# One transformer layer on one core: scores for the exponentials in four column tiles, and an order that keeps products of one kind together

## The reference, cut to what matters

```python
x = x + attention(layernorm(x))      # below
x = x + ffn(layernorm(x))            # ffn: fp4_linear(silu(gate) * up), width 704

# attention, per batch element and head
q, k = rope(xn @ Wq.T + bq), rope(xn @ Wk.T + bk);  v = xn @ Wv.T + bv
att = where(causal, q @ k.T / 4, -inf)          # 2048 x 2048
y = softmax(att) @ v
return concat_heads(y) @ Wo.T + bo
```

## Time and profile before

| | |
|---|---|
| median of 3 runs | 1375.17 us (1373.97 to 1376.26) |
| the profiled execution: its time | 1375.57 us |
| its span, first to last instruction | 1373.7 us |
| PE busy | 1315.7 us, 96% of the span |
| DVE busy | 1094.7 us, 80% |
| ACT busy | 792.5 us, 58% |
| POOL busy | 471.4 us, 34% |
| mean granted TensorE clock | 0.981 of full speed |

### The profile page before, as it was taken

How to read it: one execution, slowest core, us unless ns; L and a number is a source line. 1 busy time by engine, 2 the same in 40 slices (tenths; PEclk the granted TensorE clock), 3 DMA queues, 4 the chain that set the end, 5 groups by cost and what they waited for, 6 DMA issues and landing times.

```text
span 1373.7 us, 22507 instructions
## 1 busy us (share of the span) xinstructions
PE 1315.7 (96%) x8310; PEld 678.8 (49%) x8310; DVE 1094.7 (80%) x2242; ACT 792.5 (58%) x1691; POOL 471.4 (34%) x499
## 2 busy tenths in 40 slices
PE   7689899999999999999999999999999999999977
PEld 6455455454545554444355565555553445533345
DVE  5799889888887988787548988898888888896156
ACT  5346567765555556556775455545457665577821
POOL 2954535444342233320014566233420022300145
PEclk9779999999999999999999999999999999999989
DMA  4723222212101101010023221111101010000000
GB/s 103 185 69 93 67 66 78 55 41 53 40 5 35 32 16 32 9 29 5 25 63 85 55 70 37 29 31 39 32 9 28 24 32 12 13 2 1 9 12 16
DMA packets 56905, 56.18 MB, mean 41 GB/s; under 512 B 10062, under 2 KB 50384, under 8 KB 56784
## 3 DMA queue, kind: packets, MB, share of 16 engines
q1 hardware_dynamic: 55496, 53.66, 14.5%
q10 hardware_dynamic: 1300, 1.08, 0.3%
HBM read 37.55 MB, written 16.78 MB: 40 GB/s over the span
## 4 chain that ended last, share of the span: by engine, by line
PE 83%; DVE 10%; POOL 3%; issue 2%; ACT 1%; DMA 1%; ACTq 0%; SPq 0%; POOLq 0%; DVEq 0%
PE bank L891 18%; PE bank L870 16%; PE bank L852 16%; PE bank L903 12%; PE bank L1023 5%; PE bank L963 4%; DVE piece_max L1267 3%; PE bank L856 2%; PE bank L873 2%; PE bank L971 2%; PE bank L1014 1%; PE bank L898 1%; PE bank L985 1%; DVE c_mem L1347 1%; DVE c_mem L1339 1%
## 5 line engine op out<-in xcount | busy, mean ns | idle before, releaser
L1167 ACT ACTIVATE prob<-bank 128x512 f32<-128x512 f32 (+3 forms) x1280 | 610.2, 539 | 302.4 <-PE bank L870 164.2
L1267 DVE TENSOR_REDUCE piece_max<-bank 128x1 f32<-128x512 f32 (+3 forms) x1120 | 699.6, 664 | 70.1 <-PE bank L852 39.6
L852 PE MATMUL bank<-k_mem,q_mem 96*128 96x512 bf16 (+3 forms) x1280 | 396.9, 352 | 8.3 <-DVE piece_max L1267 6.9
L870 PE MATMUL bank<-q_mem,k_mem 99*128 99x512 bf16 (+3 forms) x1280 | 390.5, 351 | 3.5 <-DMA q_mem<-max_rows 1.6
L891 PE MATMUL bank<-prob,V 128*32 128x512 f32 (+3 forms) x2560 | 300.8, 542 | 2.0 <-ACT prob L1167 0.5
L852 PEld LDWEIGHTS bank<-k_mem,q_mem 96*128 96x128 bf16 x1280 | 122.3, 98 | 185.7 <-issue 103.8
L870 PEld LDWEIGHTS bank<-q_mem,k_mem 99*128 99x128 bf16 x1280 | 121.1, 98 | 180.7 <-issue 97.8
L1475 POOL TENSOR_TENSOR c_mem<-c_mem 128x256 f32<-128x256 f32 (+2 forms) x74 | 84.6, 1143 | 360.5 <-DVE c_mem L1351 360.5
L873 PE MATMUL bank<-mask_kq,ident_h 128*128 128x128 bf16 x512 | 105.0, 220 | 0.0
L856 PE MATMUL bank<-mask_qk,ident_h 128*128 128x128 bf16 x512 | 101.1, 224 | 0.0
L891 PEld LDWEIGHTS bank<-prob,V 128*32 128x32 f32 x2560 | 50.6, 108 | 99.6 <-issue 78.3
(11 more groups left out here) (174 smaller groups left out, 1409.3 us busy)
## 6 DMA issues: line engine op xcount, KB each, us to landing
parts_dram<-a_mem SPq DMA_DIRECT2D x13, 512.0 KB, 3.5
q_mem<-parts_dram SPq DMA_DIRECT2D x32, 192.0 KB, 3.0
k_mem<-parts_dram SPq DMA_DIRECT2D x32, 192.0 KB, 3.5
q_mem<-parts_dram SPq DMA_DIRECT2D x32, 128.0 KB, 3.1
k_mem<-parts_dram SPq DMA_DIRECT2D x32, 128.0 KB, 3.5
c_mem<-in_L_attn_x SPq DMA_DIRECT2D x30, 128.0 KB, 2.0
out<-c_mem SPq DMA_DIRECT2D x30, 128.0 KB, 1.7
a_mem<-in_L_attn_x SPq DMA_DIRECT2D x13, 256.0 KB, 3.0
```

The source lines that it names most:

```text
L852: m = pe.matmul(o, q_rows(u)[0:TERM_ROWS, h, i * P:(i + 1) * P], k_rows(k0 // CHUNK, g)[0:TERM_ROWS, h, k0 % CHUNK:k0 % CHUNK + keys], sta ...
L870: mm = pe.matmul(b[:, off:CHUNK], k_rows(j // TPC, g)[:, h, (j % TPC) * P:(j % TPC + 1) * P], q_rows(u)[:, h, off:CHUNK], start=True, stop ...
L1167: act.activation(prob[:, n % NP, off:CHUNK], bank_of("st", n)[:, off:CHUNK], ACT.Exp, scale=SCALE).then_inc(drained("st", n)[0], 1)
L1267: dve.tensor_reduce(piece_max[:, u % 2, h0:h0 + len(heads), slot], src.rearrange("p (h k) -> p h k", k=keys), AX.X, ALU.max).then_inc(drai ...
```

## The change

The scores for the exponentials are no longer one matmul with 128 weight columns, but four with 32 columns, each to its own 32 partitions of the same bank, the form that the values already have. Their masks are four too, each as wide as the last key of its quarter needs (32, 64, 96 and 128 columns of queries). The scores for maxima stay as they were. In the plan, a job of TensorE now says whether it is "divided" (exponential scores and values are, everything else isn't); a job of the other kind than the last costs 96 ns more; values cost 26 ns beside their columns instead of 235; and among jobs that could begin at once, one of the same kind as the last counts as ready 2,000 ns sooner. The cost of a score in the plan is unchanged.

```diff
--- before.py
+++ after.py
@@ -23,6 +23,8 @@
 TERM_ROWS = sum(terms for _, terms in RUNS) * HD
 ROWS = TERM_ROWS + SPLIT
 GROUP = 4
+
+COLUMNS = 32
 NGROUPS = HEADS // GROUP
 MASKED = -1.0e30
 LN_EPS = 1e-5
@@ -40,8 +42,9 @@
 HANDOVER_NS = dict(pe=195, act=200, dve=145, pool=150, sp=0, aq=0)
-DMA_TURN_NS, DMA_NS, DMA_KB_PER_NS, PV_TURN_NS = 460, 1500, 0.2, 235
+DMA_TURN_NS, DMA_NS, DMA_KB_PER_NS, DIVIDE_NS, BESIDE_NS = 460, 1500, 0.2, 96, 2000
 SOONER_NS = dict(a=0, w=0, xn=10000, s=200, st=0, pv=-100, place=1000, norm=200, c=(0, -2000), tile=1000)
 
 
@@ -77,18 +80,18 @@
         self.at, self.end, self.engine_free, self.begun = {}, {}, {}, {}
         self.bank, self.turn, self.turns = {}, {}, {b: 0 for b in banks}
         self.spare, self.bank_free = list(banks), {b: 0.0 for b in banks}
-        self.jobs, self.now, self.running, self.moved = [], 0.0, None, 0.0
+        self.jobs, self.now, self.running, self.moved, self.divided = [], 0.0, None, 0.0, False
 
     def start(self, job, sooner=0.0):
 
-        self.jobs.append([self.now, sooner, job, (None, [], None), 0.0])
+        self.jobs.append([self.now, sooner, job, (None, [], None, False), 0.0])
 
     def wait(self, names=(), until=None):
-        yield None, list(names), until
+        yield None, list(names), until, False
 
     def load(self, queue, name, kbytes, after=()):
 
-        yield queue, list(after), None
+        yield queue, list(after), None, False
         self.move(queue, name, kbytes, after)
 
     def move(self, queue, name, kbytes, after=()):
@@ -96,12 +99,15 @@
         self.moved = max(self.moved, self.engine_free[queue]) + kbytes / DMA_KB_PER_NS
         self.end[name] = self.moved + DMA_NS
 
-    def step(self, engine, name, ns, after=(), shares=False):
-
-        yield engine, list(after), None
-        self.do(engine, name, ns, after, shares)
-
-    def do(self, engine, name, ns, after=(), shares=False):
+    def step(self, engine, name, ns, after=(), shares=False, divided=False):
+
+
+        yield engine, list(after), None, divided
+        self.do(engine, name, ns, after, shares, divided)
+
+    def do(self, engine, name, ns, after=(), shares=False, divided=False):
+        if engine == "pe" and divided != self.divided:
+            ns, self.divided = ns + DIVIDE_NS, divided
         since = self.running[4] if self.running else 0.0
         begin = max([self.engine_free.get(engine, 0.0), since] + [self.end[a] for a in after])
         if shares and self.begun.get("pool", 0.0) <= begin < self.engine_free.get("pool", 0.0):
@@ -111,16 +117,16 @@
         self.engine_free[engine] = begin + ns
         self.end[name] = begin + ns + HANDOVER_NS[engine]
 
-    def through(self, use, ns, engine, drain_ns, after=(), drain_after=(), first=None):
-
-        yield "pe", list(after), lambda: self.spare
+    def through(self, use, ns, engine, drain_ns, after=(), drain_after=(), first=None, divided=False):
+
+        yield "pe", list(after), lambda: self.spare, divided
         b = min(self.spare, key=lambda b_: self.bank_free[b_])
         self.spare.remove(b)
         self.bank[use], self.turn[use] = b, self.turns[b]
         self.turns[b] += 1
         free = ("bank", b, self.turn[use])
         self.end[free] = self.bank_free[b]
-        self.do("pe", use, ns, [*after, free])
+        self.do("pe", use, ns, [*after, free], divided=divided)
         self.start(self.drain(use, b, engine, drain_ns, drain_after, first), self.running[1])
 
     def drain(self, use, b, engine, ns, after, first):
@@ -136,11 +142,11 @@
         self.spare.append(b)
 
     def can_go(self, job):
-        _, names, until = job[3]
+        names, until = job[3][1:3]
         return all(name in self.end for name in names) and (until is None or until())
 
     def ready(self, job):
-        engine, names, until = job[3]
+        engine, names, until, _ = job[3]
         ends = [job[0]] + [self.end[name] for name in names]
         if engine is None and until:
             ends.append(self.now)
@@ -151,6 +157,8 @@
     def goes(self, job):
         ready = self.ready(job)
         sooner = job[1]() if callable(job[1]) else job[1]
+        if job[3][0] == "pe" and self.divided == job[3][3]:
+            sooner += BESIDE_NS
         return max(ready, self.engine_free.get(job[3][0], 0.0)), ready - sooner
 
     def run(self, over=lambda: False):
@@ -379,15 +387,15 @@
                 yield from plan.wait([("place", u, 2), ("key ones", c)] + room
                                      + ([("drain", "st", n - ST_IN_FLIGHT)] if n >= ST_IN_FLIGHT else []))
                 yield from plan.through(("st", n), 0.43 * (CHUNK - off) + 59 * (j >= c * TPC), "act",
-                                        52 + 0.833 * (CHUNK - off), [("place", u, 2)], room)
+                                        52 + 0.833 * (CHUNK - off), [("place", u, 2)], room, divided=True)
 
     def rehearse_values():
         for m, (u, j, off) in enumerate(steps):
             k, g = units[u]
             of = k - k % NCHUNKS + j // TPC
-            yield from plan.step("pe", ("pv", m), 1.67 * (CHUNK - off) + PV_TURN_NS,
+            yield from plan.step("pe", ("pv", m), 1.67 * (CHUNK - off) + 26,
                                  [("drain", "st", GROUP * m + 3), ("drain", "v", (of * TPC + j % TPC) // PAIR)]
-                                 + ([("o copy", u - 1)] if j == 0 and u else []))
+                                 + ([("o copy", u - 1)] if j == 0 and u else []), divided=True)
             if m == final_step[u]:
                 yield from plan.step("act", ("o copy", u), 493, [("pv", m)] + ([("oT", u - 1)] if u else []))
                 plan.start(rehearse_normalising(u), SOONER_NS["norm"])
@@ -867,10 +875,14 @@
                         at.wait_ge(key_ones_loaded[j // TPC], 16)
                         masked = j >= c * TPC
                         b = take("st", n)
-                        mm = pe.matmul(b[:, off:CHUNK], k_rows(j // TPC, g)[:, h, (j % TPC) * P:(j % TPC + 1) * P],
-                                       q_rows(u)[:, h, off:CHUNK], start=True, stop=not masked)
-                        if masked:
-                            mm = pe.matmul(b[:, off:off + P], ident_h[:, :], mask_kq[:, :], start=False, stop=True)
+                        for k0 in range(0, P, COLUMNS):
+                            first = (j % TPC) * P + k0
+                            mm = pe.matmul(b[k0:k0 + COLUMNS, off:CHUNK], k_rows(j // TPC, g)[:, h, first:first + COLUMNS],
+                                           q_rows(u)[:, h, off:CHUNK], start=True, stop=not masked)
+
+                        for k0 in range(0, P if masked else 0, COLUMNS):
+                            mm = pe.matmul(b[k0:k0 + COLUMNS, off:off + k0 + COLUMNS], ident_h[:, k0:k0 + COLUMNS],
+                                           mask_kq[:, 0:k0 + COLUMNS], start=False, stop=True)
                         mm.then_inc(filled("st", n)[0], 1)
 
             def values():
@@ -888,7 +900,7 @@
                         at.wait_ge(o_copied, u)
                     for h in range(GROUP):
                         v0 = (g * GROUP + h) * VW
-                        mm = pe.matmul(O[32 * h:32 * h + 32, off:CHUNK], V[:, of % V_SLOTS, j % TPC, v0:v0 + 32],
+                        mm = pe.matmul(O[COLUMNS * h:COLUMNS * (h + 1), off:CHUNK], V[:, of % V_SLOTS, j % TPC, v0:v0 + 32],
                                        prob[:, (GROUP * m + h) % NP, off:CHUNK],
                                        start=(j == 0), stop=(m == final_step[u]), skip_group_check=True)
                     mm.then_inc(pv_added, 1)
```

## The result

| | before | after |
|---|---|---|
| median, us | 1375.57 (1373.97 to 1376.26) | 1416.41 (1416.14 to 1422.54) |
| ratio, 95% interval | | 1.0309 (1.028 to 1.0339) |
| profiled execution's span, us | 1373.7 | 1420.7 |
| mean granted clock of TensorE | 0.981 | 0.967 |
| runs of tile form, counted from TensorE's order of instructions | 343 | 383 |

The kernel became 3.1% slower, 41 us. The profiled execution of after is the longest of its four, 6 us above their median, so its rows show a little too much. A "run" here is a stretch of tile-form products on TensorE with no whole-array product between them, as in the prediction; executions of a kernel are not meant. The runs count every stretch of products with at most 32 weight columns, transposes of the maxima included, in the whole kernel.

What follows compares the result with a forecast made beforehand. The prediction took dense TensorE to bound the mixed stretches and ScalarE those where scores run alone. Its only term, (329 - 282) runs x 0.23 us = +10.8 us, gave 1386 us; 8-in-10 range 1360 to 1418.

Steps and rivals of the forecast that it cites:

- mixed stretches: 60 to 675 and 708 to 1256 us: all work mixed, TensorE dense; a microsecond added there costs nearly one.
- the step of 2.07 us unchanged where scores run alone: 675 to 708 and 1256 to 1312 us: ScalarE's four exponentials set each step's pace, before and after.
- A score in four tiles costs its columns: Exponential scores: four tiles stream at once, so 512 columns still take 0.217 us.
- The bound of +54 us: Upper bound if each of 1,280 scores and 512 masks waits 0.03 us for weights; nothing was taken.
- Supply of instructions at nothing: 5,376 more loads and matmuls priced at nothing; rival at 0.06 us a pair: +164 us, 1550, chance 0.06 including tiles not streaming together.
- The price of a turn, 0.23 us: Each tile-form run on TensorE: about 0.10 us in, 0.10 out, 0.03 once for first weights.
- R: Number of tile-form runs in mixed stretches: 282 now, estimated 329 after, from 3.4 pieces for each whole-array run.
- the ring: At most three scores in flight, so a run of scores alone ends after three.
- gain nothing: 38 steps of ScalarE-bound stretches: lose turns, about 9 us of TensorE time, which TensorE then waits.
- Fragments: Rival: waits and narrow diagonal steps cut runs to 2.5 scores, +39 us, 1414; chance 0.09 shared with VectorE dry.
- VectorE dry: Rival: VectorE loses 0.1 us in each of 329 tile runs, +33 us on top, 1419; chance 0.09 shared with Fragments.
- Longer runs: Rival: runs of a whole step or more, 4.5 scores giving 1368 us, 5.25 giving 1360; chance 0.33.

Runs made afterwards that it cites:

- the fastest kernel: The changed kernel with waiting steps also given the 2,000 ns, four scores of each kind in flight, and maxima transposes called divided: 1359.82 us, ratio 0.9893.
- the tie mended: The changed kernel, but in the plan jobs that only wait for something get the 2,000 ns too: 1395.05 us, ratio 1.0154.
- the two orders of 1451 and 1456 us: The 1359.82 us kernel with 1,000 ns instead of 2,000: 1451.32 us; the kernel before with four scores of each kind in flight: 1456.03 us.

## Why the prediction was right in direction and wrong in size

The forecast was +10.8 us; it became +41. The time lies inside the wide range and outside the likeliest case's own (1379 to 1400). The step that failed is "TensorE as dense as before in the mixed stretches, and the step of 2.07 us unchanged where scores run alone": the sum had turns as its only term and put at nothing what the new order makes late. TensorE's idle time rose from 58.0 to 88.3 us and its busy time at the lower clock from 34.0 to 69.1, which cost some 30 and 17.5 us of the 47 between the profiled executions.

- **A score in four tiles costs its columns: right.** The kernel with only the order changed and after itself have the same time (1416.77 and 1416.41). The bound of +54 us is out. Three pairs of kernels have the same order and differ in form alone: 489 runs more and +92.6 us, 33 more and -0.4, 73 fewer and -10.5. With 0.19 us a run and nothing for the form they would be +93, +6 and -14.
- **Supply of instructions at nothing: right.** A dense place of the fastest kernel, four products of 32 weight columns at each row:

```profile
562.29 0.24 PE L882 MATMUL bank<-q_mem,k_mem 99*32 99x128 bf16 x4
562.36 0.23 PE L886 MATMUL bank<-mask_kq,ident_h 128*32 128x32 bf16 x4
562.39 0.26 PE L882 MATMUL bank<-q_mem,k_mem 99*32 99x128 bf16 x4
```

  The eight products of the first two rows start within 0.10 us (562.29 to 562.39), with their loads, 0.013 us each against the rival's 0.06. It isn't only a burst: 64 in a row, from 1233.62 us of this kernel on, start 0.024 us apart. The rule of 62 ns in the Trainium skill ("TensorE: Matmul & The Clock Gate", Part 1) isn't seen in any of the runs.
- **The price of a turn, 0.23 us: right to a fifth.** 0.19 over 489 runs with nothing else changed, 0.14 over 73. Where the order changes with the number, the quotient is anything from 0.04 (2,000 to 500 ns) to 0.31 (500 to 0 ns), because the order's own cost is in it.
- **R: too low.** The 343 and 383 are of the whole kernel. Counted as the forecast did, in mixed stretches and without the runs that are transposes of maxima alone, before has 281 (282 in the forecast) and after 365, not 329: 3.1 pieces to a whole-array run instead of 3.4. That is 84 more instead of 47, and by the forecast's own sum +19 us instead of +10.8. Part of the 84 is work that moved: the stretches where scores run alone had 39 runs before and none after. Over the whole kernel 40 runs more would be 8 to 9 us of the 41, and the table above doesn't show even these. That 40 is close to 47 is chance.
- **"The step of 2.07 us unchanged where scores run alone", "gain nothing": wrong, twice.** The step became 2.46 us. I took the three scores ahead of the values as given by the ring, and costed the new preference only as a saver of turns. It also decides ties, and it decided them against the scores. Mended, the step is 1.98 us and 21.4 us come back. Only 15 steps of after are that long, some 7 us at 0.48 each; the other 14 lie mostly in mixed stretches, as less idle time and less of the lower clock, and weren't measured by themselves. And "what TensorE saves it waits" is wrong too: with the tie mended a step is 0.10 us shorter than before, so the turn was on the path there.
- **No cost for holding jobs back: wrong.** The sum had no term for what is made late by a preference of 2,000 ns. The tie mended, the kernel is still 20 us above before (19.2 in the profiled executions), with 14.1 us more idle time and 6.5 us more from the lower level. With 500 ns idle time is within 5 us of before's (62.9 against 58.0) and the time at the lower level is below it (28.4 against 34.0). So they come with the preference; which held-back job makes which wait is argued from single rows (4.67 us for the maxima's DMA; waits for `max_parts` of 12.7 us in all against 8.6) and isn't shown.
- **Rivals.** Fragments (1414) comes nearest in time and is wrong in mechanism: runs were not cut. VectorE dry has the right idea, a wait that comes from the order, at the wrong engine for after; it is what happens in the two orders of 1451 and 1456 us. Longer runs (1360) needed a ring of four and a mended order. Then R = 258 gave 1359.82; the forecast had R = 215 for this time and by its sum 1370 for 258, so part of the agreement is luck.

## What to carry to other kernels

A change of the order has two sides, the turns that it is meant to save, and what it makes late; the second was the larger here, so cost a preference in a planner as you would cost a wait, and ask of each pair of jobs that can tie which one goes first now. To see which side a loss is on, split the span into idle time, busy time at the lower clock, and the rest, before you count anything else. Test the form and the order apart: the old order with the new form, and the new order with the old form, took two kernels and settled where the 41 us were. And where one constant of a planner moves the time by 90 us, compare two kernels only after each had its own order looked for.

## What the runs showed of the hardware

- Four products of 32 weight columns, each to its own 32 partitions, take the time of one product of 128 weight columns: same order, 1416.41 and 1416.77 us, with 5,376 more loads and matmuls, and 0.23 us from start to start at 690.56.
- Between one form and the other TensorE loses 0.09 to 0.10 us on the way in and 0.10 to 0.11 on the way out (561.37 to 561.85 above); over a whole kernel 0.19 us a run of the form (92.6 us for 489).
- A stretch in which TensorE waits for reductions shows a granted clock of 0.64, and the next 50 us, with longer waits for other engines, 0.58, so it is for most of the time at the lower of its two levels (1.2 and 2.4 GHz), where the 50 us before it, 49.06 of them busy, show 1.00. An order that lets TensorE wait is paid for twice: by the wait, and by the products that then run at the lower level (three scores in 1.40 us at 299.42 of after, in 0.75 at 691.65).
